# Two state-space layers on one core: sums put off behind projections, B and C split by TensorE and ScalarE, a fourth gate by GpSimd

## What is computed

```python
# layer 0: 8 directions (4 orders, forward and backward), 16 states per channel
x_dbl = einsum('bkdl,kcd->bkcl', xs, x_proj_weight)
dts, Bsx, Csx = split(x_dbl, [R, R + N], axis=2)
delta = softplus(einsum('bkrl,kdr->bkdl', dts, dt_projs_weight) + bias)
h = exp(delta * A) * h + (delta * u) * B        # one step of 1024
y = sum_n h[n] * C[n]
# layer 1: 4 directions that share their weights
log_decay = cumsum(dt * A);  decay = exp(log_decay)
h = decay * cumsum(dt * u * B / (decay + 1e-12))
y = sum_n h[n] * C[n]
```

## Time and profile before

| | us |
|---|---|
| median of 3 runs | 15882.23 (15869.29 to 15883.01) |
| profiled execution | 15876.26 |
| its span | 15874.5 |
| busy: VectorE (DVE) | 14803.2, 93% |
| busy: GpSimd (POOL) | 13733.8, 87% |
| busy: TensorE (PE) | 12727.5, 80% |
| busy: ScalarE (ACT) | 8869.0, 56% |
| granted TensorE clock, mean | 0.942 |

### The profile page before, as it was taken

The page is one execution under the profiler, slowest core; times in us unless marked ns, Lnnn a source line. Parts: engine busy times, 40 slices in busy tenths (PEclk is TensorE's granted clock), DMA queues, the critical chain, the costliest instruction groups (busy, mean ns, idle before and its releaser), DMA issues.

```text
span 15874.5 us, 127286 instructions
## 1 busy us (share of the span) xinstructions
PE 12727.5 (80%) x41904; PEld 7576.5 (48%) x41904; DVE 14803.2 (93%) x8766; ACT 8869.0 (56%) x8411; POOL 13733.8 (87%) x5860
## 2 busy tenths in 40 slices
PE   6887888878788787887878878788788887888877
PEld 4553355533555335553355533555335553355533
DVE  8998999989999899998999989999899998999988
ACT  4445744457444574546754467444674446744466
POOL 7997889978899788997789977899779997799977
PEclk9999999999999999999999999999899998999989
DMA  5552256522555225652255522565226552265522
GB/s 183 204 203 100 82 183 207 201 98 81 188 208 202 92 80 191 209 203 90 77 197 205 203 90 75 199 207 204 87 72 207 202 204 86 72 207 203 203 82 74
DMA packets 688853, 2443.63 MB, mean 154 GB/s; under 512 B 78396, under 2 KB 100168, under 8 KB 688200
## 3 DMA queue, kind: packets, MB, share of 16 engines
q1 hardware_dynamic: 688200, 2435.49, 44.6%
HBM read 2419.45 MB, written 15.73 MB: 153 GB/s over the span
## 4 chain that ended last, share of the span: by engine, by line
POOL 29%; PE 28%; DVE 18%; issue 15%; DMA 7%; ACT 2%; SPq 0%; DVEq 0%; POOLq 0%; ACTq 0%
POOL room L987 21%; PE bank L573 15%; DMA room<-bc_rows 7%; POOL room L996 4%; DVE room L1233 4%; DVE room L1162 4%; PE bank L552 4%; DVE room L1170 4%; PE bank L520 3%; DVE room L1253 3%; POOL room L963 2%; PE bank L393 2%; DVE u L1113 1%; PE bank L482 1%; PE bank L644 1%
## 5 line engine op out<-in xcount | busy, mean ns | idle before, releaser
L987 POOL TENSOR_TENSOR room<-room 128x1024 f32<-128x1024 f32 x3072 | 7168.1, 2365 | 92.2 <-DMA room<-bc_rows 87.1
L1162 DVE TENSOR_TENSOR_SCAN room<-bank,room 128x1024 f32<-128x1024 f32 x3072 | 6935.5, 2275 | 122.7 <-ACT bank L766 71.5
L520 PE MATMUL bank<-room,identity 128*128 128x256 f32 x24576 | 6016.5, 390 | 215.9 <-DVE room L1170 206.1
L520 PEld LDWEIGHTS bank<-room,identity 128*128 128x128 f32 x24576 | 4766.2, 195 | 1439.1 <-issue 295.5
L766 ACT ACTIVATE bank<-room,a 128x1024 f32<-128x1024 f32 x3072 | 3403.3, 1115 | 3564.2 <-DVE room L1162 3549.7
L573 PE MATMUL bank<-room,identity 128*128 128x512 f32 x6144 | 3143.4, 660 | 982.7 <-DVE room L1253 902.1
L1233 DVE TENSOR_TENSOR_SCAN room<-bank,room 128x1024 f32<-128x1024 f32 x1536 | 3439.1, 2274 | 45.2 <-POOL room L1033 28.8
L1170 DVE TENSOR_TENSOR room<-room,bank 128x1024 f32<-128x1024 f32 x2360 | 2821.0, 1195 | 288.3 <-PE bank L493 278.6
L573 PEld LDWEIGHTS bank<-room,identity 128*128 128x128 f32 x6144 | 1259.9, 211 | 2807.9 <-issue 1423.6
L493 PE MATMUL bank<-parts,pick_row 96*128 96x512 bf16 x4720 | 1440.3, 387 | 1274.7 <-DVE room L1170 1242.4
L1033 POOL TENSOR_TENSOR room<-room 128x1024 f32<-128x1024 f32 x768 | 2314.6, 3036 | 57.2 <-ACT room L841 27.7
(11 more groups left out here) (104 smaller groups left out, 8980.1 us busy)
## 6 DMA issues: line engine op xcount, KB each, us to landing
room<-bc_rows SPq DMA_DIRECT2D x4552, 512.0 KB, 4.4
wx<-in_w_x SPq DMA_DIRECT2D x65, 162.0 KB
bc_rows<-xdbl SPq DMA_DIRECT2D x72, 128.0 KB, 4.1
pictures<-in_x SPq DMA_DIRECT2D x8, 768.0 KB, 10.9
out_x<-pictures SPq DMA_DIRECT2D x8, 768.0 KB, 5.2
win<-in_w_in SPq DMA_DIRECT2D x16, 288.0 KB, 7.0
room<-in_w_in SPq DMA_DIRECT2D x16, 288.0 KB, 6.0
room<-in_w_out SPq DMA_DIRECT2D x16, 288.0 KB, 6.3
```

What stands on the lines that cost most here:

```text
L520: ins = nc.tensor.matmul(dst[line][part], identity[:, :], src[line][part], start=(i == 0 and n == 0 and line == 0), stop=(n == N - 1 and l ...
L987: nc.gpsimd.tensor_tensor(source0[:, g % SOURCES, :], du0[:, j, :], b_ring0[:, g % BROWS, :], ALU.mult).then_inc(S["source"], note("source ...
L1162: nc.vector.tensor_tensor_scan(run(state0[:, g % STATES, :]), run(whole(DECAY0[g % 2])), run(source0[:, g % SOURCES, :]), 0.0, ALU.mult, A ...
```

## The change

In layer 0 the unit (2, 2) of each direction but the last goes to GpSimd as in the other passes, and the `dt` piece of pass 2 moves from unit 5 to unit 2. The bfloat16 parts are no longer made by GpSimd: `remainders` lets TensorE form x minus its parts in the WORK banks, once for parts two and three and once for part three, and ScalarE copies them out (`second_part`, `third_part`), for half of the columns each at the units 8 and 11 of pass 2. For the first direction they stand in `head0`. `begin_sums` is the load of y cut out of `sum_states`. In TensorE's order the sums of units 0 and 1 of a pass come one unit later, and so does the sum that met a remainder. `norm` for the gate is done by ScalarE (`normalize_again`) with a shift that VectorE prepares. The store of the last picture moves from unit 3 to unit 12, `residual` from unit 1 to 3. In layer 1 GpSimd does all four gate products in 12 of the 48 units (`m % 4 == 2`), and TensorE adds a product by C one unit later.

The diff, cut to what matters:

```diff
+def all_by_pool(m):
+    return m % 4 == 2
...
-    return n in ((5, 8, 11) if j == 2 and i < K - 1 else (2, 5, 8, 11))
+    return n in (2, 5, 8, 11)
...
-    if n == (2 if j == 0 else 5) and ahead < PASSES:
+    if n == (5 if j == 1 else 2) and ahead < PASSES:
         return "dt", ahead // J, ahead % J
     if i < K - 1 and (j, n) in QUARTERS:
         return "xd", i + 1, QUARTERS.index((j, n))
+    if i < K - 1 and j == 2 and n in (8, 11):
+        return "rest", i + 1, int(n == 11)
...
+                        if c == CROWS - 1 and b > 0:
+                            sp.wait_ge(S["mm"], at("mm", ("out", 1, 1), b - 1))
...
-                    if g == 3 and b > 0:
+                    if g == 12 and b > 0:
...
                 dt_proj(b, 0, 0, 1, SPARE)
+                for h in range(2):
+                    remainders(b, 0, h)
...
+            def remainders(b, i, h):
+                wait_free(0, 1)
+                pe.wait_ge(S["p1"], at("p1", (0, i), b))
+                nc.tensor.matmul(bank[0:XR, WORK[h], :], identity[0:XR, 0:XR], xdbl[0:XR, halves(h)],
+                                 start=True, stop=False)
+                step = ("rest", i, h)
+                nc.tensor.matmul(bank[0:XR, WORK[h], :], minus[:, :], parts[:, i % 2, halves(h)],
+                                 start=False, stop=True).then_inc(S[mm(step)], note(mm(step), step))
+                nc.tensor.matmul(bank[0:2 * N, WORK[1 - h], :], identity[0:XR, 0:2 * N], xdbl[0:XR, halves(h)],
+                                 start=True, stop=False)
+                pe.wait_ge(S["p2"], at("p2", (0, i, h), b))
+                step = ("last", i, h)
+                nc.tensor.matmul(bank[0:2 * N, WORK[1 - h], :], minus_two[:, :], parts[:, i % 2, halves(h)],
+                                 start=False, stop=True).then_inc(S[mm(step)], note(mm(step), step))
+                free[0] = free[1] = ("parts", (0, i, h), b)
...
+            def sum_states(b, g):
+                i, j, n = UNITS[g]
+                kind = "weigh_pool" if by_pool(i, j, n) else "weigh"
+                pe.wait_ge(S[kind], at(kind, (i, j, n), b))
...
+            def put_off(g):
+                p = piece(g)
+                return p is not None and p[0] == "rest"
...
                     if g >= SUM_LAG and by_pool(*UNITS[g - SUM_LAG]):
                         sum_states(b, g - SUM_LAG)
-                    if 0 <= last < len(UNITS) and not by_pool(*UNITS[last]):
+                    n = UNITS[g][2] if g < len(UNITS) else N
+                    if n == 1:
+                        begin_sums(b, last)
+                    if n in (2, 3) or g >= 2 and put_off(g - 1):
+                        sum_states(b, g - 2)
+                    if 0 <= last and n not in (1, 2) and not put_off(g) and not by_pool(*UNITS[last]):
                         sum_states(b, last)
...
                 for m in range(len(UNITS1)):
+                    if m > 1:
+                        add_weighted(b, m - 2)
                     if m > 0:
                         pe.wait_ge(S["weigh1"], at("weigh1", UNITS1[m - 1], b))
-                    add_direction(m, 0)
-                    add_direction(m, 1)
-                    if m > 0:
-                        add_weighted(b, m - 1)
-                    add_direction(m, 2)
-                    add_direction(m, 3)
+                    for q in range(Q):
+                        add_direction(m, q)
+                add_weighted(b, len(UNITS1) - 2)
...
+            def normalize_again(b, l, c):
+                act.wait_ge(S["shift"], at("shift", l, b))
+                nc.scalar.activation(xz[l][:, c, :], xT(b)[:, c, :], ACT.Identity, scale=rstd[:, l, c:c + 1],
+                                     bias=shift[:, l, c:c + 1]).then_inc(S["xz"], note("xz", (l, c)))
...
+            def second_part(b, i, h):
+                step = ("rest", i, h)
+                act.wait_ge(S[mm(step)], at(mm(step), step, b))
+                nc.scalar.activation(parts[0:64, i % 2, halves(h)], bank[0:64, WORK[h], :], ACT.Copy).then_inc(
+                    S["p2"], note("p2", (0, i, h)))
+            def third_part(b, i, h):
+                step = ("last", i, h)
+                act.wait_ge(S[mm(step)], at(mm(step), step, b))
+                nc.scalar.activation(parts[0:32, i % 2, halves(h)], bank[0:32, WORK[1 - h], :], ACT.Copy).then_inc(
+                    S["parts"], note("parts", (0, i, h)))
...
+                    if g == 1:
+                        for h in range(2):
+                            second_part(b, 0, h)
+                            third_part(b, 0, h)
+                    if g in (1, 2) and b > 0:
+                        take_out1(b - 1, g - 1)
...
+                    if g < len(UNITS) and (i, j) == (K - 2, 1) and n in (9, 11):
+                        normalize_again(b, 0, n // 11)
...
+                    if m > 0 and all_by_pool(m - 1):
+                        act.wait_ge(S["scan1"], at("scan1", (*UNITS1[m - 1], 1), b))
+                    elif m > 0:
...
-                    last_gate(m)
+                    if not all_by_pool(m):
+                        last_gate(m)
...
-                        gates(m + 2, 2)
+                        gates(m + 2, *((2, 3) if all_by_pool(m + 2) else (2,)))
                     if n == 2 and j + 1 < J:
                         columns(j + 1)
+                    if j == J - 1 and n in (8, 9):
+                        normalize_again(b, 1, n - 8)
...
-            def first_rest(b, i):
-                pool.wait_ge(S["p1"], at("p1", (0, i), b))
-                nc.gpsimd.tensor_tensor(rest, xdbl[0:XR, :], parts[:, i % 2, :], ALU.subtract).then_inc(
-                    S["r1"], note("r1", (0, i)))
-            def third_part(b, i):
-                pool.wait_ge(S["source"], at("source", (i - 1, 2, 13), b))
-                pool.wait_ge(S["p2"], at("p2", (0, i, 1), b))
-                slot = parts[64:96, i % 2, :]
-                nc.gpsimd.tensor_tensor(slot, rest[64:96, :], slot, ALU.subtract).then_inc(
-                    S["parts_pool"], note("parts_pool", (0, i)))
-                pool.wait_ge(S["parts_pool"], at("parts_pool", (0, i), b))
...
-                    for q in range(Q - 1):
+                    for q in range(Q if all_by_pool(m) else Q - 1):
...
-                    if g == 1 and b > 0:
+                    if g == 3 and b > 0:
...
-                    gate_last(m)
+                    if not all_by_pool(m):
+                        gate_last(m)
```

81 lines of the change are left out of this document (33 added, 48 removed).

## The result

The changed kernel takes 15,634.6 us (median of 4 runs, 15,626.0 to 15,642.3), the kernel before beside it 15,875.8 (15,869.2 to 15,883.0): ratio 0.9847, 95% interval 0.9835 to 0.9859. It is faster, by 241 us. The forecast was 410 us, 15,470, and the time lies 45 us above the range of 15,350 to 15,590. The profiled execution took 15,640.1 us, its span is 15,638.3. VectorE is busy 93% of it, GpSimd 88%, TensorE 83%.

The account below looks back on a forecast made before the run. VectorE sets the pace in both layers' scan stages, GpSimd close behind. Per image 22.4 us (layer 0) plus 28.8 (layer 1), times 8, is 410: from 15876 to 15466, forecast 15470 us, own range 15425 to 15515; 15350 to 15590 holds the first four.

Parts of the forecast that it names:

- Start of an image: Layer 0, first direction: remainders delay the output projection, first product near 2064; VectorE's third part (2.8) and 5.00 standstill go.
- I take 1 later: Start of an image, unit 8: between 1.3 us earlier and 3 later than before; 1 us later booked.
- Sums put off: Layer 0, pass starts: only a projection and one sum stay before the spread, 4.1 us against 4.4 at full clock.
- Waits of directions 2 to 7: Layer 0: VectorE's waits for TensorE's spread fall from 5.1 to 3.3 us a direction, 10.8 us per image over six directions.
- 1.0 booked at (0, 3): Layer 0: wait left behind a dt projection, between none and 1.7 to 1.8 us; the same at (1, 6) and (2, 3).
- The wait at (2, 6): Layer 0: VectorE's wait of up to 2.8 us goes, because its dt projection moves to (2, 2).
- the rule that the prediction set against the change: TensorE: short idle times between matmul groups going from bank to bank, as the remainders are, make its clock swing; no size.
- rivals 2 and 4: 2: remainders' low clock eats the sums' gain, 15568, chance 0.19; 4: TensorE stays low from (2, 8), 16138, 0.03.
- Products by C at (2, 2), the normalisation: Layer 0: one product to GpSimd in seven directions saves VectorE 7.8 us per image; normalisation to ScalarE saves 4.9.
- Layer 1: Stage from 578.0 to 549 us, net 28.8 saved per image, with GpSimd becoming its bound.
- 8 x 1.9 (meetings): Layer 1: GpSimd gate products that meet a step sum, booked in GpSimd's 537 us of work.
- rival 3: Layer 1: GpSimd meets more two-operand VectorE work or waits for ScalarE's fourth gate; half the gain stays, 15585, chance 0.11.

Follow-up runs that it names:

- short projections: All three mends plus the dt projection cut in two in all three blocks: 15,382.8 us; with the first direction's sums put off too, 15,416.1 us.
- the first edit: Changed kernel with the sums of units 0 and 1 back in the old order in the first direction only: 15,594.8 us, ratio 0.9827.
- three mends: Changed kernel with three edits together: first direction's old sum order, its B and C parts made as before, step-sum ones from PSUM: 15,541.7 us, ratio 0.9789.

## Why the prediction was wrong, step by step

The steps that failed are the balance of the start of an image, the sums put off in the first direction (a wait and a fall of the clock that stood in no term), the size of the waits left in directions 2 to 7, and in layer 1 the meetings, which were booked for GpSimd and fell on VectorE. The first direction, the first two of these together, is the largest miss, 74 us.

**Start of an image.** "I take 1 later" for unit 8; it came 6.9 later in the second image. The exchange itself was forecast well: a first product 18 us behind the first scan, measured 20.4. The balance behind it failed. It took VectorE's third part (2.8) off, though that stood in front of the first product, inside time that now is waiting. Even with my own numbers the start was 9.7 - 5.0 = 4.7 later. The rest is the 2.4 us, and 2.5 of stretched residuals, less what lay inside the wait at unit 3. Giving the parts and the place of the residuals back took 60 us off.

**Sums put off.** The prediction spoke of "TensorE loads y (1.7), sums unit 0" for every pass. In the first direction no y is loaded, and TensorE stood idle for 3.91 us where the sum had been; in the prediction's sum this direction has only the product at (2, 2) and the 1 us of the start. Undoing it in that direction took 40 us off (33 beside short projections). Of the first direction's 73 us, 33 lie in passes 1 and 2, nearly all of them in pass 2 (51.0 us before, 54.6 after, on the mean of the images); pass 1 stood at 53.9 us in five images of the kernel before too, and with the start of the image as before it takes 51.1 though its sums are put off.

**Waits of directions 2 to 7.** Forecast from 5.1 us to 3.3 each, measured over 48 from 4.7 to 3.9: 41 us saved instead of 86. Two terms failed. 5.1 came from one image, the mean of all is 0.4 lower. And 1.0 booked at (0, 3) was 1.6; (1, 6) with 0.7 and (2, 3) with 1.2 were near. At (0, 3) putting the sums off made the wait longer (1.2 us before, 1.1 with the sums in place again), while the 0.5 us at (1, 3) went. The wait at (2, 6) went wholly (100.3 us before, 0), and the remainders cost 0.4, forecast 0.3, with no fall of the clock behind (2, 8): no unit from (2, 8) to the end of a pass has the lower level in any of the 48, which is against the rule that the prediction set against the change. So rivals 2 and 4 are out in these directions. The remainders hurt where they stand ahead of the output projection; the clock is low there, and its share is open. A direction took 150.2 us on the mean, forecast 149.6. The scans themselves took 8.5 us more over the 48 directions, a small loss that no term had.

**Products by C at (2, 2), the normalisation.** Right. VectorE's products fell by 8.1 to 8.4 us over eight images in each of seven directions (forecast 8.9), and the 40.1 us of normalisation in direction 7 are gone.

**Layer 1.** The stage came to 552.5 (forecast 549), but for another reason than forecast: VectorE bounds it. Its terms: waits before the product by C 14.9 (forecast 13.9), gates 14.4, normalisation 4.1, and a term that I did not have: the step sums, -7.6 an image. Sum 25.8, measured 25.7; the match is in part luck, since these are the second image's waits and the sum leaves out some 1.3 us of new waits before the scans and the gates. I had the meeting in hand and booked it for GpSimd alone, "8 x 1.9 (meetings)". Before, GpSimd waited for VectorE's gate in every unit. With that wait 56 of the 64 step sums started 2.1 us behind the start of a GpSimd source, 0.26 us before its end, and took 2.40 us (the eight others 4.33). In the changed kernel half of the step sums stand in units without that wait, behind units 6 and 10: they start some 0.2 to 0.9 us into an operation of GpSimd and take 4.15 us on the mean. The others, behind units 4 and 8, take 3.06. That was rival 3's mechanism with VectorE as the one that pays, at half of its price.

**Between the stages.** Forecast -2, measured -23 us. In the second image the output projection of layer 0 (L650) takes 13.47 us where it took 12.16. The clock had fallen earlier against the work: low from 14.5 to 17.9 us and from 24.7 to 34.9 us behind the last scan, before from 23.9 to 30.7. Whether all of the 21 us are of this kind was not tested.

The misses, 74 + 56 - 5 + 26 + 21 = 172, are the gap between 410 forecast and 236 measured on the spans, but for 2 us of rounding.

## What to carry to other kernels

Before work is moved off an engine, ask what its wait for the other engine was good for. VectorE's gate kept GpSimd in step, and freed of it GpSimd met the step sums at other phases. A scan of VectorE with two operands in SBUF that had to run beside GpSimd was cheaper with one of them in PSUM, here a single element (74 us). Where TensorE's clock falls now and then, cutting the long piece of work in two halves, three units apart, did more (136 us alone) than any order of the sums around it; the same cut into neighbouring units brought nothing.

## What the runs showed of the hardware

- VectorE's operation with two SBUF operands and GpSimd's take turns, and the one that comes second waits: 4.19 us instead of 2.3 on VectorE, 4.36 instead of 2.36 on GpSimd. The time goes by how much of the other is left: 2.40 us with 0.26 left, 4.19 with 2.04 left. With VectorE's second operand in a bank both run side by side, at 2.29 and about 2.36.
- The gains of three edits did not add: 40 + 60 + 74 alone, 93 together. Layer 1 kept its gain; in layer 0 the granted clock was low at other units (a pass of 53.9 us that with the first edit alone took 51.5).
- An unedited stretch can change by 22 us over eight images (the second direction: 1210 us in the changed kernel, 1233 without the fourth gates, 1231 with three mends). That is as large as some terms of the sum.
